# The decay products of a masked attention in one undivided instruction, one over the root of each head's sum as the scale of the last exponential, and new step lists

## What is computed

```python
scores = einsum('bhqd,bhkd->bhqk', q, k) / sqrt(dk)
sc = softmax(where(dam, scores, NEG)) * mask * dam
distcum = cumsum(sc, axis=-1)
disttot = sum(sc, axis=-1, keepdims=True)
dist = sqrt(clip((disttot - distcum) * pos, 0.0, None))
gamma = -softplus(gammas)
te = clip(exp(dist * gamma), 1e-05, 100000.0)
scores = softmax(where(mask & dam, scores * te, NEG))
out = einsum('bhqk,bhkd->bhqd', scores, v)
```

## Time and profile before

| | us |
|---|---|
| median of 3 runs | 3373.02 |
| lowest and highest of them | 3371.89 and 3376.10 |
| the profiled execution | 3372.7 |
| its span, first to last instruction | 3371.0 |
| PE busy | 2990.0 (89%) |
| DVE busy | 2802.8 (83%) |
| ACT busy | 2715.9 (81%) |
| POOL busy | 775.8 (23%) |

### The profile page before, as it was taken

One profiled execution on the slowest core, in us unless ns is written; L12 is line 12 of the kernel. 1 busy time (PEld: TensorE's weight loads), 2 busy tenths in 40 slices (PEclk: granted clock), 3 DMA queues, 4 the chain that ended last, 5 costly groups with the idle time before them and its releaser, 6 DMA issues.

```text
span 3371.0 us, 71476 instructions
## 1 busy us (share of the span) xinstructions
PE 2990.0 (89%) x19520; PEld 2204.6 (65%) x19520; DVE 2802.8 (83%) x5825; ACT 2715.9 (81%) x10244; POOL 775.8 (23%) x1111
## 2 busy tenths in 40 slices
PE   2689999999999999999999999999999998999986
PEld 1466676666676666676666666666666666666664
DVE  3688988888988888988888988888988888988883
ACT  1688888888888888888888888888888887888883
POOL 1212222222222222222222221222221222221221
PEclk9799999999999999999999999999999999999998
DMA  5000101000101000101100001000101101001100
GB/s 160 20 25 25 32 25 33 27 26 25 30 25 33 27 26 25 30 25 33 28 26 25 29 24 33 29 26 25 28 24 33 29 28 29 24 24 33 29 17 10
DMA packets 166407, 101.66 MB, mean 30 GB/s; under 512 B 36697, under 2 KB 165709, under 8 KB 166221
## 3 DMA queue, kind: packets, MB, share of 16 engines
q1 hardware_dynamic: 166220, 99.97, 10.4%
HBM read 56.26 MB, written 10.01 MB: 20 GB/s over the span
## 4 chain that ended last, share of the span: by engine, by line
PE 55%; DVE 19%; issue 12%; SPq 4%; ACT 3%; DMA 2%; POOL 1%; DVEq 0%; ACTq 0%; POOLq 0%
PE gen_ps L623 17%; PE gen_ps L755 13%; PE gen_ps L709 6%; PE gen_ps L673 4%; SPq L556 4%; PE gen_ps L690 3%; DVE E L920 3%; PE scores_ps L664 2%; ACT X L802 2%; PE scores_ps L652 2%; DVE X L929 2%; PE gen_ps L718 2%; PE gen_ps L631 2%; PE gen_ps L684 2%; DVE res L964 2%
## 5 line engine op out<-in xcount | busy, mean ns | idle before, releaser
L802 ACT ACTIVATE X<-X,nm 128x128 f32<-128x128 f32 x1536 | 596.0, 405 | 56.7 <-DVE nm L945 55.8
L802 ACT ACTIVATE E<-scores_ps,nm 128x128 f32<-128x128 f32 x1536 | 542.3, 406 | 24.2 <-DVE nm L912 24.0
L912 DVE TENSOR_REDUCE nm<-scores_ps 128x8 f32<-128x1024 f32 x320 | 390.3, 1220 | 182.0 <-PE scores_ps L652 113.6
L623 PE MATMUL gen_ps<-f_buf,up_w 128*128 128x256 f32 x2048 | 466.1, 383 | 0.8 <-ACT f_buf L459 0.8
L1052 POOL TENSOR_SCALAR_AFFINE_SELECT X<-X 128x1024 f32<-128x1024 f32 x192 | 211.2, 1100 | 1100.8 <-DVE X L939 1100.0
L755 PE MATMUL gen_ps<-down_w,hidden 128*128 128x256 f32 x2048 | 459.7, 379 | 0.0
L802 ACT ACTIVATE X<-scores_ps,nm 128x128 f32<-128x128 f32 x1024 | 362.3, 400 | 116.6 <-issue 60.9
L673 PE MATMUL gen_ps<-ident,X 128*128 128x128 f32 x2560 | 380.0, 283 | 79.2 <-ACT xv_t L476 39.8
L929 DVE SCALAR_TENSOR_TENSOR X<-E,rz,decay 128x128 f32<-128x128 f32 x1536 | 431.0, 350 | 3.7 <-DVE E L920 0.5
L920 DVE TENSOR_TENSOR_SCAN E<-chain,E 128x1024 f32<-128x1024 bf16 x192 | 429.8, 2238 | 0.0
L623 PEld LDWEIGHTS gen_ps<-f_buf,up_w 128*128 128x128 f32 x2048 | 382.7, 191 | 70.5 <-issue 21.9
(11 more groups left out here) (124 smaller groups left out, 5491.7 us busy)
## 6 DMA issues: line engine op xcount, KB each, us to landing
k_diag<-k_f SPq DMA_DIRECT2D x768, 32.0 KB, 1.9
xk_diag<-xk_f SPq DMA_DIRECT2D x1024, 8.0 KB, 1.8
ctx_f<-in_ctxT SPq DMA_DIRECT2D x32, 256.0 KB, 3.2
ctx_t<-in_ctx SPq DMA_DIRECT2D x32, 256.0 KB, 2.8
x_f<-in_xT SPq DMA_DIRECT2D x32, 256.0 KB, 2.6
x_t<-in_x SPq DMA_DIRECT2D x32, 256.0 KB, 2.6
cx_f<-in_ctxT SPq DMA_DIRECT2D x32, 256.0 KB, 2.7
out<-out_t SPq DMA_DIRECT2D x32, 256.0 KB, 2.2
```

The lines of the kernel that those rows point to most:

```text
L623: mm = nc.tensor.matmul(ps[:, i * T:(i + 1) * T], w[:, k, c * P:(c + 1) * P], src[:, k, :], start=(k == 0), stop=(k == C - 1))
L802: a = nc.scalar.activation(dst[:, cols], src[:, cols], ACT.Exp, bias=minus_max[:, h:h + 1], accum_out=sums[:, h:h + 1])
L912: nc.vector.tensor_reduce(nm1[:, UNIT[u], :], unit_heads(scores_ps[SLOT[u]][:, :]), AX_X, ALU.max, negate=True).then_inc(max1_done, 1)
```

## The change

**x** (L929 before) becomes one product of E and decay over all 1024 columns, without 1/z1. The reciprocal (L918) goes, and with it one of the two counts of scan_done for each unit.

**zroot** is new, on POOL: z1 of 8 columns to the power of minus one half, and then times minus one, into rz1. It waits for exp1, and its own second instruction waits for its first.

**effect** becomes 8 exponentials, one for each head, with that column of rz1 as the scale. It now waits for zroot as well as for root.

**The tables** are all new: the order on every engine, the PSUM tiles (BANKS), and which engine reads what. ACT now reads 10 halves of probabilities in a turn and 2 results of up, where it read 14 and 6; the read of q is DVE's and not ACT's, of k(0) DVE's and of k(1) ACT's, of v(2) ACT's and of v(0) DVE's. Of five turns ACT reads three (four before). DVE has what ACT lost.

```diff
-TENSOR = [(1, ("up", 0, 2)), (1, ("up", 0, 3)), (0, ("k", 0)), (1, ("down", 0)), (2, ("att", (3, 0, 0))),
...
+TENSOR = [(1, ("scores", (2, 0))), (1, ("up", 0, 0)), (1, ("scores", (2, 1))), (1, ("up", 0, 3)), (0, ("k", 0)),
...
+POOL = [(1, ("select", (2, 0))), (1, ("select", (2, 1))), (1, ("dev", 0, 2)), (2, ("widen", (3, 1, 1))),
+    (0, ("zroot", (0, 1))), (1, ("widen", (2, 1))), (1, ("widen", (2, 0))), (0, ("zroot", (0, 0))),
+    (0, ("select", (0, 0))), (0, ("select", (0, 1))), (1, ("dev", 2, 1)), (0, ("widen", (0, 0))),
...
-        neg_half = sb("neg_half", [P, G])
+        neg_half = sb("neg_half", [P, UH])
...
             def effect(now, d, u):
-                x = X[:, X_SLOT[u], :]
+
+                x, n = X[:, X_SLOT[u], :], UNIT[u]
+                act.wait_ge(zroot_done, zroot_order.upto(now, d, ("zroot", u)))
                 act.wait_ge(root_done, root_order.upto(now, d, ("root", u)))
-                nc.scalar.activation(x, x, ACT.Exp, scale=-1.0).then_inc(te_done, 1)
+                for i in range(UH):
+                    cols = slice(i * S, (i + 1) * S)
+                    a = nc.scalar.activation(x[:, cols], x[:, cols], ACT.Exp, scale=rz1[:, n, i:i + 1])
+                a.then_inc(te_done, 1)
...
                 dve.wait_ge(exp1_done, exp1_order.upto(now, d, ("exp1", u)))
-                nc.vector.reciprocal(rz1[:, UNIT[u], :], z1[:, UNIT[u], :]).then_inc(scan_done, 1)
...
-                dve.wait_ge(scan_done, dist_order.upto(now, d, ("dist", u)) * 2)
-                for i in range(UH):
-                    ins = nc.vector.scalar_tensor_tensor(out=X[:, p, i * S:(i + 1) * S],
-                                                         in0=E[:, E_SLOT[u], i * S + 1:(i + 1) * S + 1],
-                                                         scalar=rz1[:, UNIT[u], i:i + 1], in1=decay[:, l, i, :],
-                                                         op0=ALU.mult, op1=ALU.mult)
-                ins.then_inc(x_done, 1)
+                dve.wait_ge(scan_done, dist_order.upto(now, d, ("dist", u)))
+                nc.vector.tensor_tensor(X[:, X_SLOT[u], :], E[:, E_SLOT[u], 1:UW + 1],
+                                        decay[:, u[0], :, :].rearrange("p h s -> p (h s)"), ALU.mult).then_inc(x_done, 1)
...
+            def zroot(now, d, u):
+
+                n = UNIT[u]
+                wait_apart(pool, exp1_done, exp1_order.upto(now, d, ("exp1", u)))
+                nc.gpsimd.tensor_tensor(rz1[:, n, :], z1[:, n, :], neg_half[:, :], ALU.pow).then_inc(zpow_done, 1)
+                wait_apart(pool, zpow_done, zroot_order.upto(now, d, ("zroot", u)))
+                nc.gpsimd.tensor_scalar(rz1[:, n, :], rz1[:, n, :], -1.0, None, ALU.mult).then_inc(zroot_done, 1)
```

75 lines of the change are left out of this document (37 added, 38 removed), and 61 rows, old and new, of tables (SCALAR, TENSOR, VECTOR).

## The result

The changed kernel takes 3498.5 us, the kernel before on the same chip 3373.8: a ratio of 1.037 (95% interval 1.0352 to 1.0388), 125 us or 3.7% slower. Forecast were 3424, 51 us slower. The direction and the mechanism were right; the loss is more than twice what the sum gave.

What follows compares the result with a forecast made beforehand. No engine was far ahead; a ring of two stretches bound each turn. Long stretch 67.9 + 3.8 + 3.4 + 2.6 = 77.7 us, 4.0 more, way back 2.4 less: 3373 + 51 = 3424 us, range 3320 to 3505.

Steps and rivals of the forecast that it cites:

- The new wait: ACT at effect(0, 0) waits for POOL's zroot, queued behind another root and two widens: 3.4 us, ends 2.4 and 5.2.
- The long stretch: From the start of exp1(2, 0) to the end of exp2(1, 1): 77.7 us forecast, 4.0 more than 73.7.
- the way back: From the end of exp2(1, 1) to exp1(2, 0), 26.8 us before: 2.4 us less, through turn(1, 1)'s read and o(1).
- ACT's work: ACT's busy time between exp1(2, 0) and exp2(1, 1): 67.9 us before, net 3.8 us added.
- the power of 128x8: First instruction of zroot on POOL: taken as 1.3 us, between 0.8 (fixed cost) and 2.2 (cost per column).
- The other waits in the long stretch: ACT's waits between exp1(2, 0) and exp2(1, 1) besides the one at effect(0, 0): 5.8 - 3.2 = 2.6 us remain.
- the stand of 3.42 us at turn(2, 2): PE's wait behind down(2) for tok(2, 2), with half clock after it, 1.0 + 0.3 us lost; was to go.
- The turn taken for all 32: One middle turn of 100.5 us stood for all; 1.6 us longer each, 51 us over 32 turns.
- The covered wait: Rival: ACT reaches effect(0, 0) later than POOL's list, wait 0.5 us, turn 1.3 us shorter, 3331 us; chance 0.27.
- The slow power and shared port: Rival: POOL's power takes 2.2 us, DVE and POOL block each other, turn 5.2 us longer, 3539 us; chance 0.15.
- the change cancels itself: Rival: the wait at effect(0, 0) is near 1.8 us and what goes pays for it, 3373 us; chance 0.08.
- the ring: Two mutually dependent stretches, exp1(2, 0) to exp2(1, 1) and back, 73.7 and 26.8 us; no turn can be shorter than both.

Runs made afterwards that it cites:

- e7: Changed kernel with POOL's root of (0, 0) moved ahead of both layer 2 widens but still behind the root of (0, 1): 3423.9 us.
- e14: Changed kernel with 15 useless 128x256 matmuls on PE, all before att(2, 0): 3464.4 us.
- e1: Changed kernel with four POOL entries reversed: root of (0, 0) first, root of (0, 1) last, the two widens between them swapped: 3302.7 us.
- e11: Kernel with the early root of (0, 0) (3303 us), with the root of (0, 1) also moved ahead of the layer 2 widens: 3319.1 us.
- e9: Kernel before with POOL's two root instructions added as idle work nobody waits for, in e5's POOL list: 3387.4 us.
- e4: Changed lists and undivided product, but DVE's reciprocal as scale of eight logarithms, one exponential of 1024, no root on POOL: 3432.3 us.
- e3: Code of the kernel before on the six tables of the changed kernel, POOL's without the roots: 3369.8 us.
- e10: Kernel with the early root (3303 us), its effect as one activation of 1024 with constant scale -1, the root unused: 3239.4 us.
- e5: Code of the changed kernel on the tables of the kernel before, roots put into POOL's list where they hold nobody up: 3528.3 us.
- e2: Kernel before with the effect's last exponential as eight activations of 128 columns with constant scale, in place of one of 1024: 3399.7 us.

## Why the prediction came out as it did

**The direction and the mechanism were right.** The new wait is where it was put, at effect(0, 0), ended by POOL's multiplication, with the copy for att(2, 1) behind it and PE in order behind that. The long stretch was forecast as 77.7 us and was 80.6; the way back as 24.4 and was 24.39; ACT's work as 71.7 and was 71.3.

**The term that failed is the new wait: 3.4 us forecast, 5.8 measured**, above the end of 5.2 as well. It has two sides. POOL had been given 6.4 us from the end of exp1(0, 1): 1.8 for the first root, 2.8 for the widens, 1.8 for the second root. It took 3.2, 3.0 and 2.1 (to the start of the effect 8.4). ACT was ready after 2.6 us, and not 2.9. Two causes stand behind POOL's 2.0 us:

- the power of 128x8 takes 1.67 us and not 1.3: with its multiplication a root takes 2.1 undisturbed and not 1.8, twice. The value chosen between the bounds from the earlier trace rows was too near the fixed cost. The widens took 0.3 us more than the two of the earlier trace rows, and 0.7 more than the 2.38 us of e7, where they meet no product of DVE;
- the sharing between POOL and DVE falls on the root itself. The multiplication takes 0.25 us undisturbed and 1.35 when it meets the running sum. The forecast had taken this from the earlier trace rows for the widens alone, and only in the rival, with 1.0 us; in the sum it stood at nothing, without a reason.

These 2.4 us are 77 us over 32 turns, and 51 + 77 = 128, close to the measured 125. That closeness is luck, since three smaller errors stand against each other:

- **The other waits in the long stretch** were forecast as 2.6 us and are 3.5. The half clock behind the new stands belongs here: the forecast had it behind the stand of 3.42 us at turn(2, 2), and did not ask what a new stand at att(2, 1) would do. It is worth 34 us in the changed kernel (e14).
- **ACT's work** is 0.4 us less than forecast.
- **The turn taken for all 32** was the wrong measure. The turn of the earlier trace rows has 100.5 us where the mean of 28 is 101.0, and the turn cut from the changed kernel has 105.0 where the mean is 104.7. So the 4.5 us between these two are 3.7 us in the mean.

Together the three come to about 0.3 us a turn.

**What was right in it.** The product is one instruction of 1.24 us in the mean (1.0 to 1.2 forecast, so just above); the eight activations are 0.293 us apart (0.29); turn(1, 1) on PE waits 0.92 us and its read follows; behind down(2) no wait over 1 us is left and no slow window, where it was 3.42 us. ACT is busy 86.5 us in a turn and DVE 85.9 (87 to 88 and 87 forecast). The estimate from the Trainium skill, ScalarE: Activation LUTs, What ACT_TABLE_LOAD costs, was given as 1.41 us more for each unit (its figures give 1.40); measured are 2.44 - 1.06 = 1.38, and the forecast had 1.36.

**The rivals.** The covered wait had 74.8 + 24.4 us and 3331 us of time. It is e1: 74.15 + 24.38 us, 3303 us. So its turn was right within 0.7 us, and its bound, faster as soon as the wait is under 1.8 us, agrees with runs on both sides: e11 and e1 wait 0.6 us at most and are faster, e7 waits 2.9 us and is slower. The slow power and shared port had the sizes (a wait of 6.2 in its sum) nearer than the forecast had, and its place for the sharing was half right: DVE holds up POOL, but the running sum went from 2.24 to 2.28 us only, and the 0.8 us for that did not come. Even the 0.04 is not the root's: with roots and the reciprocal kept (e9) it is 2.24, as it is with neither roots nor eight products (e4), and only kernels without the reciprocal have 2.28 or 2.29. Why these are slower no run shows. The case that the change cancels itself did not come; what comes nearest to it are the new lists with the old code (e3).

**What the sum had taken for granted and the runs do not bear out in general** is that ACT's added work counts in full on the ring, and DVE's saving for nothing (e3 and e10 above). ACT's work comes near that in the last step of each row above (e4, e5), and is about a quarter in the steps below (e2, and e10 against e1). In the changed kernel the count may have held because the wait for POOL made ACT the one on whom the rest of the long stretch waited; no run shows that.

## What to carry to other kernels

When a step goes to a third engine, its place in that engine's queue is worth more than its own time: here the step costs 13 us as idle work (e9), and standing last of four, behind a piece whose own input comes 3.9 us later, costs 196 (with the two widens in the other order). Put a new producer at the head of its queue at the moment when its input is ready, and sum the queue from there with each piece at its disturbed duration, since the same event that releases it also releases the other engine's longest instruction. Before a loss is put down to a change, its code and its order of instructions should be run apart: here either alone gained nothing or lost, and together with four entries exchanged they gain 2.2%.
